# FFN down projection: a residual that the DMA accumulates in HBM against a residual added by VectorE

## The reference

```python
x = x + 0.5 * _L0_ffn_ref(_layernorm(x), w_gate_up, w_down)   # stage 1
x = x + _L0_attn_ref(_layernorm(x), B, C, D)                  # stage 2
x = x + 0.5 * _L0_ffn_ref(_layernorm(x), w_gate_up, w_down)   # stage 3
...
def _L0_ffn_ref(h_shard, w_gate_up, w_down):                  # 2048 -> 2 x 8192 -> 2048
    gate, up = split(einsum('bsh,oh->bso', h_shard, w_gate_up), 2)
    return einsum('bsi,hi->bsh', silu(gate) * up, w_down)
```

## Time and profile before

| what | us |
|---|---|
| median of 2 runs | 9695.69 (9428.28 and 9963.11) |
| the profiled execution | 9411.82 |
| its span, core 7, the slowest | 9410.5 |
| spans of the eight cores | 9291.8 to 9410.5 |
| PE busy | 6591.9 (70%) |
| chain that ended last: wdn loads | 7% |

### The profile page before, as it was taken

One profiled execution on the slowest core, in us unless ns is written; L12 is line 12 of the kernel. 1 busy time (PEld: TensorE's weight loads), 2 busy tenths in 40 slices (PEclk: granted clock), 3 DMA queues, 4 the chain that ended last, 5 costly groups with the idle time before them and its releaser, 6 DMA issues.

```text
span 9410.5 us, 69695 instructions; the slowest of 8 cores (9291.8 to 9410.5 us)
## 1 busy us (share of the span) xinstructions
PE 6591.9 (70%) x28213; PEld 2799.6 (30%) x28213; DVE 1312.3 (14%) x1973; ACT 895.9 (10%) x1420; POOL 642.7 (7%) x972
## 2 busy tenths in 40 slices
PE   5999999926665763644999999936666672535535
PEld 2444444412222321211444444412222230102101
DVE  4010101000000003004110101000000004343254
ACT  2000000000000002102000000000000002112220
POOL 0000000000000001111000000000000000110202
PEclk8999999968887886877999999968878786657665
DMA  3323232273334336244222222263333336391655
GB/s 61 59 57 59 57 59 56 57 156 56 65 71 104 56 61 121 39 54 64 59 57 59 57 59 57 59 161 61 63 81 92 64 60 113 39 144 28 73 110 72
DMA packets 263629, 676.51 MB, mean 72 GB/s; under 512 B 21888, under 2 KB 74240, under 8 KB 246928
## 3 DMA queue, kind: packets, MB, share of 16 engines
q0 software_dynamic: 166912, 453.90, 31.0%
q1 hardware_dynamic: 82576, 192.98, 7.3%
q10 hardware_dynamic: 13824, 25.17, 0.9%
HBM read 840.60 MB, written 268.44 MB: 118 GB/s over the span
## 4 chain that ended last, share of the span: by engine, by line
PE 65%; DMA 15%; DVE 8%; SPq 3%; issue 3%; ACT 2%; another core or an unknown queue 2%; ACTq 1%; POOL 1%; DVEq 0%; POOLq 0%
PE ps L280 37%; PE ps L369 10%; PE ps L371 10%; DMA WBUF<-wdn 7%; DVE XBF L56 5%; SPq L135 3%; DMA res_a<-RESG 2%; DMA WBUF<-ct 2%; PE ps L454 2%; DMA res_b<-RESG 1%; ACT RESG L56 1%; ACTq L135 1%; PE ps L421 1%; PE ps L806 1%
## 5 line engine op out<-in xcount | busy, mean ns | idle before, releaser
L280 PE MATMUL ps<-XBF,WBUF 128*128 128x512 bf16 x16384 | 3544.7, 380 | 61.0 <-DVE XBF L56 61.0
L280 PEld LDWEIGHTS ps<-XBF,WBUF 128*128 128x128 bf16 x16384 | 1604.5, 98 | 2000.7 <-issue 73.2
L369 PE MATMUL ps<-BIGB,WBUF 128*128 128x512 bf16 x2048 | 863.8, 422 | 1210.8 <-DMA WBUF<-wdn 869.2
L371 PE MATMUL ps<-BIGB,WBUF 128*128 128x512 bf16 x2048 | 859.0, 419 | 0.0
L369 PE MATMUL ps<-XBF,WBUF 128*128 128x512 bf16 x2048 | 779.1, 380 | 105.4 <-DMA XBF<-h_scr 105.4
L56 DVE TENSOR_TENSOR HEV<-TMPF,ps 128x512 bf16<-128x512 f32 x512 | 351.9, 687 | 3175.3 <-PE ps L280 3134.5
L371 PE MATMUL ps<-XBF,WBUF 128*128 128x512 bf16 x2048 | 778.9, 380 | 0.0
L369 PEld LDWEIGHTS ps<-BIGB,WBUF 128*128 128x128 bf16 x2048 | 218.2, 107 | 1531.5 <-issue 1340.1
L56 ACT ACTIVATE TMPF<-ps 128x512 f32<-128x512 f32 x512 | 305.8, 597 | 3178.3 <-PE ps L280 3141.3
L56 DVE TENSOR_SCALAR TMPF<-ps 128x512 f32<-128x512 f32 x24 | 16.6, 692 | 4198.4 <-PE ps L214 2479.6
L56 DVE TENSOR_TENSOR XBF<-XBF,TMPF 128x512 bf16<-128x512 bf16 x768 | 531.5, 692 | 112.9 <-ACT TMPF L56 32.7
(11 more groups left out here) (141 smaller groups left out, 2111.6 us busy)
## 6 DMA issues: line engine op xcount, KB each, us to landing
WBUF<-wgu POOLq DMA_DIRECT2D x256, 512.0 KB, 6.0
WBUF<-wdn POOLq DMA_DIRECT2D x128, 1024.0 KB, 14.7
h_scr<-HEV SPq DMA_DIRECT2D x128, 512.0 KB, 5.5
res_a<-RESG POOLq DMA_DIRECT2D x64, 512.0 KB, 6.2
res_b<-res_a SPq DMA_DIRECT2D x8, 4096.0 KB, 85.5
res_b<-RESG POOLq DMA_DIRECT2D x128, 256.0 KB, 6.8
res_a<-res_b SPq DMA_DIRECT2D x8, 4096.0 KB, 84.2
XBF<-res_a POOLq DMA_DIRECT2D x48, 512.0 KB, 87.6
```

Of the source, the lines that this page charges most:

```text
L280: last = t.matmul(banks[tc][:], wsl[:, k * 128:(k + 1) * 128], XBF[:, k * T + tc * TC: k * T + (tc + 1) * TC], start=(k == 0), stop=(k == ...
L369: t.matmul(b0[:], wsl[:, ib * 128:(ib + 1) * 128], hsrc[:, 0:512], start=st_, stop=sp_)
L371: last = t.matmul(b1[:], wsl[:, ib * 128:(ib + 1) * 128], hsrc[:, 512:1024], start=st_, stop=sp_)
```

## The change

The four HBM-to-HBM copies and POOL's wait for them are gone. Instead, ACT's queue loads the residual of the output block (128 x 1024 fp32, 512 KB) from `res_src` into the half of `RESG` that the block will use, once the store that last read this half has landed (`ssl`). VectorE makes `bank * 0.5 + residual` in place in `RESG` with two scalar_tensor_tensor operations in the place of ScalarE's two copies. SP waits for VectorE and stores the 512 KB to `res_dst` as a plain write. PE waits for VectorE (`ev`) instead of ScalarE (`sc`) before it reuses a pair of banks.

```diff
@@ emit_l0ffn @@
         h_stored = (self.hsl[0].n, self.hsl[1].n)
-        for i in range(4):
-            self._dma(q, self.cpy, res_dst[:, i * TC:(i + 1) * TC],
-                      res_src[:, i * TC:(i + 1) * TC])
-        g.wait_ge(self.cpy.h, self.cpy.n)
...
                     if pos_h == 0 and (dblk >= 2 or tc2 > 0):
-                        t.wait_ge(self.sc.h, dn_sc[dblk % 2])
+                        t.wait_ge(self.ev.h, dn_sc[dblk % 2])
...
                 mm_done = wd_mm[1]
-                oslot = self.RESG[:, (dblk % 2) * 1024:(dblk % 2 + 1) * 1024]
-                s.wait(self.mm, mm_done)
-                if dn_st[dblk % 2]:
-                    s.wait(self.asl[dblk % 2], dn_st[dblk % 2])
-                s.activation(oslot[:, 0:512], b0[:], AF.Copy, scale=0.5)
-                s.activation(oslot[:, 512:1024], b1[:], AF.Copy, scale=0.5)
-                dn_sc[dblk % 2] = s.tok
-                g.wait_ge(self.sc.h, dn_sc[dblk % 2])
+                rslot = self.RESG[:, (dblk % 2) * 1024:(dblk % 2 + 1) * 1024]
+                if dblk >= 2 or tc2 > 0:
+                    self.nc.scalar.wait_ge(self.ssl[dblk % 2].h, dn_st[dblk % 2])
+                rtok = self._dma(self.nc.scalar, self.rsl[dblk % 2], rslot,
+                                 res_src[dblk * 128:(dblk + 1) * 128, cs2])
+                v.wait(self.mm, mm_done)
+                v.wait(self.rsl[dblk % 2], rtok)
+                v.scalar_tensor_tensor(rslot[:, 0:512], b0[:], 0.5, rslot[:, 0:512],
+                                       OP.mult, OP.add)
+                v.scalar_tensor_tensor(rslot[:, 512:1024], b1[:], 0.5,
+                                       rslot[:, 512:1024], OP.mult, OP.add)
+                dn_sc[dblk % 2] = v.tok
+                q.wait_ge(self.ev.h, dn_sc[dblk % 2])
                 dn_st[dblk % 2] = self._dma(
-                    g, self.asl[dblk % 2],
-                    res_dst[dblk * 128:(dblk + 1) * 128, cs2], oslot,
-                    accum=True)
+                    q, self.ssl[dblk % 2],
+                    res_dst[dblk * 128:(dblk + 1) * 128, cs2], rslot)
```

## The result

The changed kernel is faster: the ratio to the kernel before is 0.867, with a 95% interval of 0.859 to 0.875. The profiled execution took 8222.98 us where that of before took 9411.82, so 1188.8 us are gone; the forecast was 1197 less, 8215. The medians of all runs are 8506.16 (11 runs, 8205.78 to 8943.35) and 10037.1 (10 runs); they include executions in which cores of one die or both showed a lower granted clock, which the ratio leaves out, and where the profiled execution of an experiment has that on one die, the cores of the other die are read.

What follows compares the result with a forecast made beforehand. The prediction took the order of POOL's program, not the DMA rate, as the limit. Stalls 869, clock 140, start 179.5 and stage end 8 make 1197 us off 9411.8: 8215 us, range 8130 to 8630, chance 0.78.

Steps and rivals of the forecast that it cites:

- The stalls: Down part, output block boundaries: PE's 60 waits for wdn, 14.5 us on average, all go, 869.2 us.
- The lone load: Down part: a wdn load issued alone lands in 9.4 us, hidden under the other half-group's 13.8 us.
- The clock: Down passes: without the 60 stalls, PE's restarts at the lower clock, 2.3 us each, go, 140 us.
- Rival C: Down passes, now dense, stay at a granted clock of 0.83: 363 us more, 8578 us; chance 0.09.
- The start: Start of down parts, stages 1 and 3: without copies, 80 us to the second half-group, 179.5 us gained together.
- The boundary between passes: Start of a down part's second pass: PE's idle time of about 71 us was left unchanged in the sum.
- What was added: Per output block, two VectorE operations (1.4 us), a load and a store (about 5.7 us): no cost, bound 1.4 per stage.
- The end of stage 1: Last store lands 7.3 us after evacuation starts instead of 11.9: 4.6 us gained, 8 with stage 3.
- The failed step: Profiled execution to median: should half the later runs be slow, the median would be some 3% above 8215.
- B: Down part: a lone weight load takes 15.9 us, longer than the half-group, so blocks last 30.0: 8355 us; chance 0.08.
- D: Down part: matmuls held at the lower clock level, 1.2 GHz, 1725 us more: 9940 us, slower; chance 0.02.
- E: Block boundaries: loads still go out late because PE's last group holds POOL; only start and end gain: 9224 us; chance 0.03.

Runs made afterwards that it cites:

- the mere wait: Changed kernel plus only a POOL wait for VectorE's output ahead of the next block's weight loads, the store staying on SP; 9028.5 us.
- the two kernels with delays: Changed kernel with four or twelve small POOL operations ahead of each down weight load; four took 8215.0 and 8333.7 us, twelve 8612.2 us.
- order-only kernel: Kernel before, with POOL issuing each accumulating store behind the next block's first weight load; 8471.8 us on core 1, 9396.4 before.
- kernel with twelve delays: Changed kernel with twelve small POOL operations ahead of each weight load of the down part, 9.7 us of delay; 8612.2 us.
- the kernel with the store on POOL: Changed kernel with its plain store, and the wait for VectorE ahead of it, back on POOL; 9117.1 us.
- the version with chunks: Changed kernel loading h into SBUF earlier, with a semaphore for each 16 blocks of h instead of 32; lowest of six executions 8110.3 us.

## Why the prediction was right or wrong

**The stalls.** Right: 60 waits of 14.5 us went, all 869.2. That the order of POOL's program was the reason is shown from both sides, by the move in the kernel before and by the mere wait in the changed one. Core 7, which the prediction read, had the longest waits; over the eight cores they were 848 us.

**The lone load.** 9.4 us were estimated from half the size and the spacing of pairs; the median over all 128 is 9.5. By pass it spreads more than that: 8.8 in the first of stage 1, 11.0 in the first of stage 3. With a slowest of 13.2 the cover was thinner than the estimate made it look, but it held. That the median came so near is partly luck: the estimate had no store beside the load, and with the loads moved away from the store they landed in 8.4 and 7.8 (the two kernels with delays).

**The clock.** Right: the surplus of 37.4 us per pass is now 1.7 (444.4 less 442.7), near the one restart of 2.3 that was left in. Rival C did not come in this execution: 0.99 to 1.00 in the passes. Here the rule of the Trainium skill (TensorE: Matmul & The Clock Gate, the peak-current limiter) would have meant 0.81 in a dense stretch, and these rows do not agree with it. Other rows of this case do, in part. In the order-only kernel's trace core 7 ran stage 1's gate and up at just this level, with 6107 matmuls in 1600 us where core 1 has 7415 (same columns as the stretches above; core 1, then core 7):

```profile
200.00:1800.00 1600.00, 1600.00 (x7415) 725.34 (x7413) 159.49 (x232) 138.54 (x232) 61.30 (x116) 1.00 0.29 58
```

```profile
200.00:1800.00 1600.00, 1600.00 (x6107) 663.43 (x6106) 131.97 (x192) 113.58 (x191) 50.21 (x95) 0.81 0.25 48
```

It was a pair of cores, not a die: core 6 was at 0.81 with core 7 while cores 4 and 5 of the same die stood at 1.00, and in stage 3 (4600 to 5200) it was the other way round. So the level of that rule does occur here, and it comes and goes with the same code; what brings it was not found.

**The start.** Sized at 80 us from the last gate/up matmul to the second half-group; measured 84.7 in stage 1 (68.57 of idle time, 13.8 and 2.3) and 73.6 in stage 3. Together 158 against 160. The number fits, the way to it does not, and that is luck. The prediction had the first half-group run beneath the loads and the second one wait for the last of them, 80 us on. In fact POOL's loads of `BIGB` landed no sooner than 68.6 us after the last gate/up matmul, the second half-group then waited for nothing, and the 16.1 us of the first came on top. The transfer was shorter than the 80 us (it ran at 275 GB/s, not 255), and the half-group was not hidden: two errors that cancel.

**The boundary between passes.** The sum left it at 71 and 67 us. It became 67.9 and 61.4: 9 us that no term had. One of the two weight loads now goes out 13.8 us before the pass ends, so 1 MB less is moved in that time; that this is the whole reason was not tried.

**What was added.** VectorE's pair takes 1.49, not 1.4. The store was put at 5.7 us and lands in 9.1 at the median: mis-sized by 60%. Within a pass it goes out 1.3 us behind a weight load; at the end of a stage, without such a neighbour, it took 5.8 and 4.8. It cost nothing where 48 us of slack were. The end of stage 1 now takes 7.7 us from VectorE's start to the release of the barrier, 4.2 less than before where 4.6 were forecast. The share of the DMA engines was forecast at 0.50 and is 0.51 to 0.56. The pages count 840.60 MB read from HBM in both kernels and 268.44 MB written before against 234.88 now: the copies' 33.6 MB of writing are gone, and reads of the accumulating stores do not show in these counts.

**The sum.** 1197 forecast, 1188.8 measured between the slowest cores. Core by core the gain is 1110 (core 6) to 1282 (core 7), and the mean of the eight is 1190. That the slowest core lies so near the mean is partly luck: I had read core 7 alone. By the last down matmul of stage 3, core 7 has gained 1231 us and core 6 1179; the rest of the spread, some 119 of 171 us, arises in later stages, which the change does not touch. Its cause was not looked for.

**The failed step.** It is the one that ties the profiled execution to the median: "Should half of the later runs be like the higher one, the median would be some 3% above my number". From two runs I took the median before at 9696, with 9963 as the higher kind. Over ten runs the median before is 10037, 6.6% above the profiled execution, and five of the ten took over 10100. The measured ratio of 0.867 put on that median is 8701 us, above the upper end of 8630, and the forecast's own ratio of 8215 / 9411.8 = 0.873 gives 8761. So the allowance of 3% should have been 6.6%. The plain median after, 8506, is 3.5% above the number forecast and inside 8130 to 8630, but it comes from a set in which five of the eleven runs took under 8230, and before only two of ten were as near to the lowest. The terms of the sum for the profiled execution are not touched by it. Why a run of the same kernel comes out at 9427 or at 10492 stays open.

**Rivals.** B: no, the load stayed under 13.8; its formula is shown by the kernel with twelve delays. C and D: not in the profiled execution. E: no; POOL's loads go out at their slot's own release.

## What to carry to other kernels

A transfer behind a waiting instruction starts when the wait ends, whatever the transfer itself waits for. So put on one queue only what becomes ready in the order in which it stands, and move the late item (an output store) to a queue where nothing urgent stands behind it; to find it, compare when a load was issued with when its buffer came free. Then check the cover: a double-buffered load pays only for what exceeds the time of the other buffer, once per pair, and the restart of PE's clock on top.

## What the runs showed of the hardware

A plain store of 512 KB took 9.1 us at the median in the changed kernel, where SP issues it 1.3 us behind a weight load. Issued just ahead of the weight loads it took 3.1 us from POOL and 2.7 from SP (the kernel with the store on POOL and the one with the mere wait). At the end of a stage, with no weight load near, it took 5.8 and 4.8. Weight loads that go out 3.6 or 9.7 us late landed in 8.4 and 7.8 us (medians of 128), those that go out at once in 9.5. So what was issued just before a transfer moved its landing by a factor of up to three here, at the same size.

Not every wait cost PE its clock, and the first matmul after a wait does not tell. In the version with chunks the matmuls after waits of 3.24 and 3.25 us all took 0.38 us, as in a dense stretch, and after one of 4.93 us they began at the lower level:

```profile
2440.45 0.59 PE L373 MATMUL ps<-XBF,WBUF 128*128 128x512 bf16 x1 [4.93 <-DMA XBF<-h_scr]
...
6027.48 0.38 PE L373 MATMUL ps<-XBF,WBUF 128*128 128x512 bf16 x1 [3.25 <-DMA XBF<-h_scr]
```

In the order-only kernel (core 1) a wait of 2.63 us cost nothing, and one of 2.22 us did: the first matmuls behind it took 0.38, and the clock fell 0.9 us later, for eight matmuls:

```profile
2879.96 0.38 PE L381 MATMUL ps<-XBF,WBUF 128*128 128x512 bf16 x1 [2.22 <-DMA WBUF<-wdn]
...
2880.82 0.63 PE L381 MATMUL ps<-XBF,WBUF 128*128 128x512 bf16 x1
```

So between 2.2 and 3.3 us the length of a wait alone did not decide it here, and what a wait cost is read from the dozen matmuls behind it.
